# Graph attention sums: the segment maximum subtracted by TensorE, one one-hot tile made by VectorE, the nodes' own logits computed in another stage

## The reference

```python
e = leaky_relu(xl[src] + xr[dst], 0.2)
logits = einsum('ehc,hc->eh', e, att)
m = segment_max(logits, dst)
ex = exp(logits - m[dst])
denom = segment_sum(ex, dst)
out = segment_sum(xl[src] * (ex / denom[dst])[..., None], dst)
```

## Time and profile before

| | us |
|---|---|
| median of 3 runs (6855.04 to 6872.8) | 6864.06 |
| the profiled execution's own time | 6867.52 |
| its span, first to last instruction | 6865.7 |
| attention sums, layer 1 (1439.6 to 1916.0) | 476.4 |
| attention sums, layer 2 (3222.8 to 3634.0) | 411.2 |
| segment maxima, layer 1 and layer 2 | 99.8, 53.1 |
| logits, layer 1 and layer 2 (171.6 to 1339.8, 1996.0 to 3169.7) | 1168.2, 1173.7 |

### The profile page before, as it was taken

One profiled execution on the slowest core, in us unless ns is written; L12 is line 12 of the kernel. 1 busy time (PEld: TensorE's weight loads), 2 busy tenths in 40 slices (PEclk: granted clock), 3 DMA queues, 4 the chain that ended last, 5 costly groups with the idle time before them and its releaser, 6 DMA issues. The chain is left out here.

```text
span 6865.7 us, 123063 instructions
## 1 busy us (share of the span) xinstructions
PE 5634.3 (82%) x35774; PEld 4549.4 (66%) x35774; DVE 3765.0 (55%) x12913; ACT 2158.0 (31%) x6967; POOL 4656.2 (68%) x4393
## 2 busy tenths in 40 slices
PE   2799999647769999985886996666666499999999
PEld 2688888546668777774775996666666355555555
DVE  6655552289975555322887445666666544344343
ACT  4233334259833333333994003222222310000000
POOL 1777777678877777777887661777777157376473
PEclk8899999779969999996997998999999799999999
DMA  5788875756634444335554884555555389999998
GB/s 198 236 283 281 277 211 159 124 108 141 139 58 105 105 103 104 84 81 49 76 76 122 289 288 139 158 157 160 158 157 158 32 291 305 300 303 301 301 305 262
DMA packets 904054, 1232.19 MB, mean 179 GB/s; under 512 B 230602, under 2 KB 640862, under 8 KB 890408
## 3 DMA queue, kind: packets, MB, share of 16 engines
q1 hardware_dynamic: 607544, 887.00, 40.4%
q0 software_dynamic: 207392, 219.55, 18.4%
q10 hardware_dynamic: 88428, 117.57, 5.0%
HBM read 987.45 MB, written 237.38 MB: 178 GB/s over the span
## 5 line engine op out<-in xcount | busy, mean ns | idle before, releaser
L1023 POOL DMA_INDIRECT ACC<-table,TABS x1760 | 1722.4, 979 | 586.7 <-issue 578.2
L1348 POOL DMA_INDIRECT BUF<-table,TABS x840 | 796.9, 949 | 615.6 <-DMA table<-ACC 260.6
L1107 POOL DMA_INDIRECT adjacency<-TABS x600 | 993.0, 1655 | 264.1 <-issue 210.2
L1023 POOL DMA_INDIRECT BUF<-table,TABS x880 | 838.1, 952 | 331.5 <-issue 331.5
L1809 PE MATMUL picked<-ident,ACC 128*128 128x128 f32 (+1 forms) x3520 | 714.1, 286 | 0.0
L2158 PE MATMUL asum<-BUF 128*128 128x144 f32 x3520 | 566.1, 306 | 164.8 <-DVE BUF L2136 160.4
L1885 DVE SCALAR_TENSOR_TENSOR BUF<-BUF,TABS,wspread 128x128 bf16<-128x128 f32 (+1 forms) x600 | 324.2, 540 | 624.0 <-issue 610.1
L2158 PEld LDWEIGHTS asum<-BUF 128*128 128x128 f32 x3520 | 480.6, 199 | 195.7 <-issue 181.5
L1808 PE MATMUL picked<-G,OH 128*128 128x128 f32 (+1 forms) x2352 | 498.7, 296 | 119.3 <-DVE G L1785 60.7
L2104 ACT ACTIVATE BUF<-iota_row,TABS 128x128 f32<-128x128 f32 x1760 | 555.2, 386 | 101.3 <-PEq L89 101.3
L1802 PE MATMUL picked<-ident 128*128 128x128 f32 x3520 | 560.0, 307 | 11.1 <-PEq L89 11.1
(11 more groups left out here) (408 smaller groups left out, 10913.4 us busy)
## 6 DMA issues: line engine op xcount, KB each, us to landing
TABS<-adjacency SPq DMA_DIRECT2D x272, 512.0 KB
BUF<-in_edge_pair SPq DMA_DIRECT2D x880, 128.0 KB
BUF<-adjacency SPq DMA_DIRECT2D x102, 1024.0 KB
BUF<-adjacency SPq DMA_DIRECT2D x204, 512.0 KB
adjacency<-zeros ACTq DMA_DIRECT2D x44, 1792.0 KB
G<-adjacency SPq DMA_DIRECT2D x136, 512.0 KB
kept<-ACC SPq DMA_DIRECT2D x220, 272.0 KB, 2.8
G<-kept SPq DMA_DIRECT2D x220, 272.0 KB
```

The source lines that it names most:

```text
L1023: po.indirect_dma_start(rows[:, slot, j, 0:width], None, tab, bass.IndirectOffsetOnAxis(ap=SRC[:, q * GT + j:q * GT + j + 1], axis=0)).the ...
L1107: po.indirect_dma_start(adj_flat, bass.IndirectOffsetOnAxis(ap=PLACE[:, k:k + 1], axis=0), TOTAL[:, k:k + 1], None, compute_op=ALU.add).th ...
L1348: po.indirect_dma_start(R[:, q % deep_ring, j, :], None, table, bass.IndirectOffsetOnAxis(ap=SRC[:, k:k + 1], axis=0)).then_inc(S(f"gather ...
```

## The change

1. Sums, the subtraction. VectorE's `less_max` goes. TensorE forms logits minus maximum in PSUM (`dif`, two banks) by two products in a row: the identity with the logits, and the stored maxima with `MINUS`, a small negative identity made once. Exp reads PSUM. `turn_max` now waits also for `exp` and, between its products, for the kept rows (`got`).
2. Sums, the one-hots. ScalarE makes three of the four tiles and VectorE the fourth (`last_hot`) in every group of layer 2 and in every fourth group of layer 1. Only the last Abs raises `gap`.
3. The own logits leave `gat_logits` and are made in `edge_max`, after its first loads are issued and before its scans, in pieces that fit into the upper half of BUF[2]; the load of the closing penalties into BUF[1], where XR lies, waits for them.

```diff
-        def gat_logits(tab, XL, XR, self_l, H, C, half):
+        def gat_logits(tab, XR, H, C, half):
...
-            Zn = area[:, :, 0:W]
-            meanwhile(None, 0, [
-                lambda: ve.tensor_tensor(Zn, XL, XR, ALU.add),
-                lambda: ve.scalar_tensor_tensor(Zn, Zn, SLOPE, Zn, ALU.mult, ALU.max),
-                lambda: ve.tensor_tensor(Zn, Zn, wide(att[:, 0:W]), ALU.mult),
-                lambda: ve.tensor_reduce(self_l, Zn.rearrange("p b (h c) -> p b h c", h=H), AX_X, ALU.add)])
-            sp.wait_ge(S("between"), 4)
...
-        def edge_max(H):
+        def edge_max(H, C, XL, XR, self_l):
...
+            W = H * C
+            beside = BUF[2][:, :, :].rearrange("p b d -> p (b d)")[:, L // 2:]
+            parts = -(-NB * W // beside.shape[1])
+
+            def own_logits():
+
+                most = -(-NB // parts)
+                for low in range(0, NB, most):
+                    at = slice(low, min(NB, low + most))
+                    n = at.stop - low
+                    z = beside[:, 0:n * W].rearrange("p (b w) -> p b w", b=n)
+                    go(ve, lambda: ve.tensor_tensor(z, XL[:, at, :], XR[:, at, :], ALU.add))
+                    go(ve, lambda: ve.scalar_tensor_tensor(z, z, SLOPE, z, ALU.mult, ALU.max))
+                    go(ve, lambda: ve.tensor_tensor(z, z, wide(att[:, 0:W], n), ALU.mult))
+                    go(ve, lambda: ve.tensor_reduce(self_l[:, at, :], z.rearrange("p b (h c) -> p b h c", h=H), AX_X, ALU.add))
...
                 ac.wait_ge(S("opens0"), 16 * H)
+                ac.wait_ge(chain[0].sem, chain[0].n)
...
             load_runs()
+            own_logits()
             load_pens()
...
-            DIF = BUF[2][:, at + RING:at + 2 * RING, 0:TH].rearrange("p r (t h) -> p r t h", h=H)
+            MINUS = BUF[2][0:TH, at + RING, 0:TH]
+
+            def by_scalar(q):
+
+                return GT - 1 if H == 1 or q % 4 == 3 else GT
...
+                dif = [psum(ps, f"dif{i}", [P, 4 * P]) for i in range(2)]
...
-                    wait(sp, S("mcol"), q - RING + 1)
+                    wait(sp, S("dif"), q - RING + 1)
...
                     wait(pe, S("mfirst"), q - 1)
-                    m = pe.matmul(mcol[slot % 2][:, 0:TH], MX[:, slot, :], ident[0:TH, 0:TH], start=True, stop=True)
-                    m.then_inc(S("mcol"), 1)
+                    wait(pe, S("exp"), q - 1)
+                    pe.matmul(mcol[slot % 2][:, 0:TH], MX[:, slot, :], ident[0:TH, 0:TH], start=True, stop=True
+                              ).then_inc(S("mcol"), 1)
+                    if q == 0:
+                        pe.wait_ge(S("minus"), 1)
+                    pe.wait_ge(S(f"got{slot}"), 16 * (turn + 1))
+                    less = dif[slot % 2][:, 0:TH]
+                    pe.matmul(less, ident[:, :], LOGIT[:, slot, :], start=True, stop=False)
+                    pe.matmul(less, MX[:, slot, :], MINUS, start=False, stop=True).then_inc(S("dif"), 1)
...
-                    for j in range(GT):
-                        ac.activation(HOT[:, slot, j, :], iota_row[:, :], ACT.Abs, scale=-1.0,
-                                      bias=LOCAL[:, bass.ds(q * GT + j, 1)]).then_inc(S("gap"), 1)
+                    for j in range(by_scalar(q)):
+                        m = ac.activation(HOT[:, slot, j, :], iota_row[:, :], ACT.Abs, scale=-1.0,
+                                          bias=LOCAL[:, bass.ds(q * GT + j, 1)])
+                    m.then_inc(S("gap"), 1)
+
+                def last_hot(q, slot, turn):
+
+                    if by_scalar(q) < GT:
+                        wait(ve, S("summed"), q - RING + 1)
+                        one_hot(HOT[:, slot], q * GT, GT - 1).then_inc(S("last_hot"), 1)
...
-                    ac.activation(RHS[:, slot, :, W:W + H], DIF[:, slot], ACT.Exp).then_inc(S("exp"), 1)
-                    ac.wait_ge(S("gap"), (q + 1) * GT)
-                    ac.activation(HOT[:, slot], HOT[:, slot], ACT.Relu, scale=-1.0, bias=1.0
-                                  ).then_inc(S("hot"), 1)
+                    ac.activation(RHS[:, slot, :, W:W + H], by_head(dif[slot % 2][:, 0:TH]), ACT.Exp
+                                  ).then_inc(S("exp"), 1)
+                    ac.wait_ge(S("gap"), q + 1)
+                    tiles = HOT[:, slot, 0:by_scalar(q), :]
+                    ac.activation(tiles, tiles, ACT.Relu, scale=-1.0, bias=1.0).then_inc(S("hot"), 1)
...
-                def less_max(q, slot, turn):
-
-
-                    ve.wait_ge(S("mcol"), q + 1)
-                    ve.wait_ge(S(f"got{slot}"), 16 * (turn + 1))
-                    ve.tensor_tensor(DIF[:, slot], by_head(LOGIT[:, slot, :]), by_head(mcol[slot % 2][:, 0:TH]),
-                                     ALU.subtract).then_inc(S("dif"), 1)
...
+                    wait(pe, S("last_hot"), early[q])
...
+                ve.tensor_scalar(MINUS, ident[0:TH, 0:TH], -1.0, None, ALU.mult).then_inc(S("minus"), 1)
...
-                pipeline(nc, [(fetch_max, 0), (fetch_rows, 1), (turn_max, 2), (ve_step(less_max), 2),
+                pipeline(nc, [(fetch_max, 0), (fetch_rows, 1), (turn_max, 2),
                               (ve_step(first_rows), 3), (ve_step(first_max), 2), (ve_step(last_rows), 3),
-                              (ve_step(weight_column), 2), (add, 5),
+                              (ve_step(weight_column), 2), (ve_step(last_hot), 2), (add, 5),
                               (flush, 0), (hots, 2), (exps, 2), (products, 4)])
```

More of the change, by code:

```diff
@@ L2064, in gat_sums @@
             MX = BUF[2][0:TH, at:at + RING, :]
-            DIF = BUF[2][:, at + RING:at + 2 * RING, 0:TH].rearrange("p r (t h) -> p r t h", h=H)
+            MINUS = BUF[2][0:TH, at + RING, 0:TH]
+            def by_scalar(q):
+                return GT - 1 if H == 1 or q % 4 == 3 else GT
+            early = [sum(by_scalar(i) < GT for i in range(q + 1)) for q in range(GROUPS)]
             by_group = head_d[0:H * TILES * P].rearrange("(h g t e) -> g t h e", h=H, t=GT, e=P)
@@ L2117, in weight_column, with first_max @@
                                        ).then_inc(S("weighted"), 1)
-                def less_max(q, slot, turn):
+                def first_max(q, slot, turn):
                     ve.wait_ge(S("mcol"), q + 1)
-                    ve.wait_ge(S(f"got{slot}"), 16 * (turn + 1))
-                    ve.tensor_tensor(DIF[:, slot], by_head(LOGIT[:, slot, :]), by_head(mcol[slot % 2][:, 0:TH]),
-                                     ALU.subtract).then_inc(S("dif"), 1)
-                def first_max(q, slot, turn):
                     ve.tensor_tensor(RHS[:, slot, :, W + H:W + 2 * H], by_head(mcol[slot % 2][:, 0:TH]),
@@ L2134, in rows @@
                     ve.wait_ge(S("exp"), q + 1)
+                    ve.wait_ge(S(f"got{slot}"), 16 * (q // RING + 1))
                     half = slice(part * GT // 2, (part + 1) * GT // 2)
@@ L2199, in gat_layer @@
             two_dense(name, H, C, K, XL, XR, tab, rstd, blend)
-            gat_logits(tab, XL, XR, self_l, H, C, half)
+            gat_logits(tab, XR, H, C, half)
             merge(MERGES[half][1])
-            edge_max(H)
+            edge_max(H, C, XL, XR, self_l)
             clear(NB * WA)
```

## The result

The changed kernel takes **7662.41 us** (median of 4 runs, 7658.1 to 7664.98), the kernel before 6860.78 in the same comparison (4 runs, the three of the prediction and one more): ratio 1.1165, 95% interval 1.1146 to 1.1185, slower. The forecast was 7679, range 7480 to 7800. The profiled execution took 7664.98 us around its span of 7663.2.

What follows compares the result with a forecast made beforehand. TensorE at 1.2 GHz was taken to bound both sums stages after the change: 220 rounds of 3.9 and 3.78 us plus filling gave +826, less 11 for the own logits, +815, so 7679 us, range 7480 to 7800.

Steps and rivals of the forecast that it cites:

- The clock: Both sums stages: forecast to stay at 1.2 GHz, since a stream of 4- to 32-column matmuls shows no rise.
- The price: TensorE's added cost per sums round at 1.2 GHz: 1.14 and 1.04 us, giving cycles of 3.9 and 3.78 us.
- the whole distance of mcol to products: Sums rounds at 1.2 GHz: 0.57 and 0.52 us from mcol's loads to the products', charged for each added product.
- The division of that distance: Sums rounds at 1.2 GHz: mcol-to-products distance split into 0.17 us per load, 0.40 and 0.35 across the shape change.
- the load-only bound: Lower bound in the sums: four added loads alone at 0.17 us, cycles of 3.46 and 3.42 us, time 7500.
- The sum: Sums stages 1714 us against 887.6 before, +826; less 11 for the own logits, +815, so 7679 us.
- the term of filling and emptying: Both sums stages: some 12 us each for filling and emptying at 1.2 GHz, on top of the 220 rounds.
- the dearest case: Upper bound in the sums: every shape change at 0.54 us, cycles of 4.20 and 4.16 us, time 7810 or so.
- the own logits out of cover: Logits and maxima stages: worst bound for the move, nothing gained and 16 us of work uncovered, +16 us.
- The own logits: Logits stages 17 and 7 us shorter, maxima stages 6 and 7 us longer: net -11 us.
- The other engines: Sums stages: VectorE and ScalarE savings beside TensorE's longer round worth nothing; POOL's transfers keep their number, with more time.
- The last rival: Faster, chance 0.07: narrow products slip under wide ones, VectorE bounds both sums stages, -45 and -40, less 11: 6768 us.

Runs made afterwards that it cites:

- the round of one shape: The changed kernel with the maxima's stationary tile padded with zero rows to 128 rows, narrow products kept: 8966.78 us against 8442.44 for the kernel before.
- The best version of the change: The changed kernel with the maxima's stationary tile padded to 128 rows and 128 moving columns in all three narrow products: 6847.18 us, ratio 0.9982 to the kernel before.

## Why the prediction was right, point by point

- **The clock.** Both sums stages stay at 1.2 GHz, as forecast. The reason given, a stream too thin to raise the clock, is borne out: at 0.50 no kernel with this round rose in over 800 us, not even when it began at 1.00. But "matmuls of 4 to 32 columns, the kind that left the clock low" is only part of it: wide products with changes of shape stay low too, and narrow ones without a change as well; only both cures together brought 1.00. Padding changes the gaps and the filled rows at once, so these runs do not settle what exactly counts, and the forecast was right without knowing it. The Trainium skill ("TensorE: Matmul & The Clock Gate", Part 1) says that the clock is set "based on how busy the PE has been recently"; here TensorE is busy 703.96 of 714.4 us by the profile and stays at half clock, so the profile's busy share cannot be read as that activity.
- **The price.** 3.9 and 3.78 us a round at 1.2 GHz; 3.91 and 3.77 measured; 2.20 at 2.4 GHz, 2.19 measured. Taking the whole distance of mcol to products for each new neighbour was right. The division of that distance was not: in the round of one shape the pairs stand 0.42 to 0.46 apart, 0.21 to 0.23 a load and not 0.17, which leaves 0.10 to 0.15 for a change and not 0.23. The two errors cancel in the sum; the load-only bound feels one of them and would be 2.79+4x0.21=3.63, an estimate, instead of 3.46. The 3.20 of the round of one shape does not test it, since there the two changes that stood before are gone as well.
- **The sum.** Sums +826 forecast, +808 measured. The largest miss is the term of filling and emptying, 12 us in each stage: 868.1 less 220x3.91 leaves 8, and 832.4 less 220x3.77 leaves 3. That is 13 of the 18; the rest is the base, the stages of before being 4.9 us longer when cut at the same barriers as these. Two bounds were added up wrongly, without effect: the dearest case comes to some 7830 us, not 7810, and the own logits out of cover to +13, not +16.
- **The own logits.** -17, +6, -7, +7 forecast; -18.2, +7.5, -9.4, +5.0 measured: -15 instead of -11. Alone, on the slower chip, the move gave -25 by the medians, with 15 inside its interval.
- **The other engines.** "If TensorE's additions were free, they would be the whole gain" is the step that was wrong, in a rival and not in the forecast. The last rival had 1.85 us for VectorE in layer 1 and 1.65 in layer 2, -45 and -40 us (its own 0.16 a round gives 35 for layer 1, and a round of 1.65 would leave the two products 0.13 us in layer 2, not 0.33). With the clock up and TensorE within its time, VectorE's round in layer 1 stayed at 2.0, since the adds are a chain, and layer 2 stayed at 412.6 behind POOL's stream, which the prediction had passed over with "keep their number and have more time": it took ScalarE for what bounds that stage. The best version of the change took 6847 us, some 80 above the rival's 6768.

## What to carry to other kernels

Before moving work off an engine, read what stands right before and behind it: an instruction that fills the wait between two dependent ones costs next to nothing, and its removal gives next to nothing. Then look for the stream that merely accompanies the stage (here POOL's 216 transfers, 405 us), for it sets the floor once the rounds get shorter, and compare the end of its last instruction with the end of the stage. And a small product is not small for TensorE: here each fp32 product of 4 to 32 columns cost 0.42 to 0.56 us at 1.2 GHz, and the two added ones cost the stage its clock; padding all three to full rows and columns cost less than leaving them narrow.

## What was not expected of the hardware

- Changes of the stationary tile's shape (32 and 128 rows) cost 0.71 us a round at 1.2 GHz, 3.91 against 3.20 us with four of them: 0.10 to 0.15 for three, 0.33 from the products back to the 32-row tile; padding with zero rows removes it.
- TensorE busy for 695.75 of 696.30 us, without a gap between loads (rounds of 3.20 us), stayed at 0.50; with 96 or 124 more moving columns in three of its seven products it rose within two rounds of products and stayed for 447 us.
- Long VectorE instructions stretch POOL's indirect transfers: beside scans of 7.55 us, 7.5 and 7.3 us where 1.55 is usual.
- POOL's 216 indirect transfers took 405 to 406 us whether the rounds beside them lasted 1.72, 1.83 or 3.77 us.
